# A two-layer graph kernel: 16-bit row pick, a reordered prologue, one-hots of two slots per compare in a ring of six, and PSUM banks by chunk size

## The reference

```
# layer 0
h = x @ W + b_W;  xi, xj = split(h)
m = xj[src] + (edge_attr @ W_e + b_We);  m = m / (in_degree[dst] + 1e-6)
x = layernorm(x + xi + segment_sum(m, dst))
# layer 1: graph convolution with self loops
h = x @ W1;  deg = in_degree + 1
out = segment_sum(h[src] * rsqrt(deg[src]) * rsqrt(deg[dst]), dst) + self loop + b
y = (out - mean(out)) * rsqrt(var(out) + eps) * gamma + beta   # over all nodes
x = layernorm(x + leaky(y, 0.01))
```

## Time and profile before

| | |
|---|---|
| timed runs, median of 3 | 941.71 us (941.57 to 946.58) |
| profiled execution, its own time | 944.12 us |
| its span | 942.3 us, TensorE clock granted 0.986 of full speed in the mean |
| TensorE busy | 892.4 us (95%), 12,235 matmul records |
| VectorE busy | 704.6 us (75%), 1,638 instructions |
| ScalarE busy | 458.9 us (49%) |
| GpSimd busy | 329.6 us (35%) |
| chain that ended last | TensorE 80%, VectorE 11%, issue 4%, ScalarE 3% |
| line 608, lo_oh | 391 instructions, 271.6 us, mean 695 ns |
| line 611, key_oh | 391 instructions, 235.8 us, mean 603 ns |

### The profile page before, as it was taken

The page is one execution under the profiler, slowest core; times in us unless marked ns, Lnnn a source line. Parts: engine busy times, 40 slices in busy tenths (PEclk is TensorE's granted clock), DMA queues, the critical chain, the costliest instruction groups (busy, mean ns, idle before and its releaser), DMA issues.

```text
span 942.3 us, 30938 instructions
## 1 busy us (share of the span) xinstructions
PE 892.4 (95%) x12235; PEld 796.3 (85%) x12235; DVE 704.6 (75%) x1638; ACT 458.9 (49%) x983; POOL 329.6 (35%) x401
## 2 busy tenths in 40 slices
PE   5768998999999999999999999999999999999995
PEld 4657887988988998989999999999988888888864
DVE  6999899999999998998888998888852111112255
ACT  4755665656665665565565565566542000000035
POOL 2224444555434453554343454344432010111100
PEclk9979999999999999999999999999999999999998
DMA  6428989897877887777687659687667897779645
GB/s 178 109 98 301 373 312 326 293 327 269 317 271 285 315 308 242 254 231 235 234 291 244 234 152 332 210 290 248 229 213 310 323 358 290 266 259 326 247 123 165
DMA packets 96765, 244.76 MB, mean 260 GB/s; under 512 B 42632, under 2 KB 64838, under 8 KB 90726
## 3 DMA queue, kind: packets, MB, share of 16 engines
q1 hardware_dynamic: 94150, 239.03, 72.2%
q0 software_dynamic: 1600, 3.28, 1.1%
q10 hardware_dynamic: 864, 0.39, 0.2%
HBM read 183.82 MB, written 58.85 MB: 258 GB/s over the span
## 4 chain that ended last, share of the span: by engine, by line
PE 80%; DVE 11%; issue 4%; ACT 3%; DMA 1%; SPq 1%; ACTq 0%; DVEq 0%
PE x_ps L868 23%; PE pair_ps L943 18%; PE pair_ps L850 12%; PE e_ps L887 9%; PE x_ps L876 9%; DVE key_oh L611 3%; DVE lo_oh L608 3%; PE j_ps L925 2%; PE pair_ps L952 1%; PE j_ps L926 1%; PE j_ps L973 1%; DMA counts_kept<-counts 1%; DVE streams L631 1%; PE u_vps L1401 1%; ACT counts L1053 1%
## 5 line engine op out<-in xcount | busy, mean ns | idle before, releaser
L1053 ACT CAST counts<-pair_ps 128x784 bf16<-128x784 f32 x391 | 314.6, 817 | 263.2 <-PE pair_ps L850 258.7
L868 PE MATMUL x_ps<-counts,xsplit 128*128 128x256 bf16 (+1 forms) x2450 | 307.8, 271 | 1.4 <-issue 1.4
L608 DVE TENSOR_TENSOR lo_oh<-counter,lo_t 128x1024 bf16<-128x1024 bf16 x391 | 271.6, 695 | 42.6 <-PE pair_ps L850 37.7
L868 PEld LDWEIGHTS x_ps<-counts,xsplit 128*128 128x128 f16 x2450 | 222.1, 98 | 31.4 <-issue 9.2
L611 DVE TENSOR_TENSOR key_oh<-counter,key_t 128x800 bf16<-128x800 bf16 x391 | 235.8, 603 | 0.0
L850 PE MATMUL pair_ps<-key_oh,lo_oh 128*128 128x100 bf16 x3128 | 207.3, 208 | 22.8 <-ACT counts L1053 13.5
L850 PEld LDWEIGHTS pair_ps<-key_oh,lo_oh 128*128 128x128 bf16 x3128 | 181.0, 98 | 39.3 <-DVE key_oh L611 17.2
L887 PE MATMUL e_ps<-streams 128*32 128x128 f32 x3528 | 108.8, 277 | 0.0
L876 PE MATMUL x_ps<-counts,zown 128*128 128x256 bf16 (+1 forms) x840 | 105.8, 269 | 0.0
L887 PEld LDWEIGHTS e_ps<-streams 128*32 128x32 f32 x3528 | 94.9, 111 | 4.9 <-issue 0.7
L943 PE MATMUL pair_ps<-streams,zown 128*128 128x256 bf16 x878 | 99.0, 273 | 0.0
(11 more groups left out here) (179 smaller groups left out, 866.0 us busy)
## 6 DMA issues: line engine op xcount, KB each, us to landing
streams<-in_edge_attr SPq DMA_DIRECT2D x196, 576.0 KB, 10.4
counts_kept<-counts SPq DMA_DIRECT2D x10, 1600.0 KB, 8.4
streams<-counts_kept SPq DMA_DIRECT2D x6, 1600.0 KB, 6.4
counts<-counts_kept SPq DMA_DIRECT2D x4, 1600.0 KB, 6.4
counts_kept<-counts SPq DMA_DIRECT2D x2, 3136.0 KB, 12.5
streams<-counts_kept SPq DMA_DIRECT2D x2, 3136.0 KB, 14.5
edst<-in_dst SPq DMA_DIRECT2D x196, 4.5 KB
streams<-in_x SPq DMA_DIRECT2D x3, 1024.0 KB, 5.4
```

What stands on the lines that cost most here:

```text
L608: dv.tensor_tensor(lo_oh[:, at % RING, :, :, :], counter[:, :, :].unsqueeze(1).to_broadcast([P, SW // 2, P, 2]), pairs(lo_t[b % 2][:, w]). ...
L868: last = nc.tensor.matmul(x_ps[:, 0, 0:n], xsplit[:, q // 2, q % 2, :], by_hi[:, q // 2, :], start=(q == 0), stop=(q == 2 * HS - 1))
L1053: a.copy(out.rearrange("p h (g n) -> p h g n", g=2), pair_ps[at % 2][:, :, 0:4 * KW].rearrange("p g (n h) -> p h g n", h=HI)[:, 0:HS]).the ...
```

## The change

- **Compares.** one_hots is called for every second s and writes both slots of the pair in one instruction per table: lo_oh 128x2048 and key_oh 128x1600. The semaphore "hot" counts pairs. The ring has 6 slots. TensorE's count, of one slot, waits for the pair that holds it.
- **Row pick.** Rows have 128 edges (HR = 128) and start at any edge. float_rows writes two tensors: the first and last element of each row in fp32 (heads, 128x2), and the row's 128 elements in bf16. The pick matrix is bf16, and find_rows is one bf16 product of 128x129.
- **Prologue.** Only the rows of blocks 0 and 1 are picked before the own products. Rows 2 and 3 are picked later: on ScalarE after own_out(2), on VectorE after make_keys(0), on TensorE after turn_keys(0). The weights are loaded by SP: wi ahead of the first piece of x, the others behind rows 2 and 3. count(0, 0) waits for two starts, count(0, 1) for four.
- **Memory.** early_in and dinv_row lie in the memory of key_oh. So the first two loads of dinv_row are issued after SP's loop and behind a wait for the last count.
- **The end.** Nine chunks have fixed places in PSUM and in the x1 buffers by their size. Five add_x1 stand ahead of add_leaky(0); add_x1(5) comes behind add_leaky(3), 6 behind 4, 7 and 8 behind 5. x1 loads are all issued before the first store.

```diff
-RING = 4
+RING = 6
-HR = 125
-R = E // HR
-ROW_MARGIN = 31
+HR = 128
+ROW_SPAN, ROW_MARGIN = P * HR, 4096
+def hot_pairs(at):
+    return -(-at // 2)
-        rows = [sb(f"rows{i}", [P, HR + 2], F32) for i in range(2)]
+        rows = [sb(f"rows{i}", [P, HR + 1], BF16) for i in range(2)]
+        heads = [sb(f"heads{i}", [P, 2], F32) for i in range(2)]
-        pick = [sb(f"pick{i}", [P, P], F32) for i in range(2)]
+        pick = [sb(f"pick{i}", [P, P], BF16) for i in range(2)]
+        spare = key_oh[:, :, :, :, :].rearrange("p r w k t -> p (r w k t)").bitcast(F32)
+        early_in, dinv_row = ([spare[:, BN * i:BN * (i + 1)] for i in k] for k in ((2, 3), (4, 5)))
...
             for b in range(2):
                 load_rows(sp, b)
+            sp.dma_start(wi, W0[:, 0:F]).then_inc(S["wi_in"], 16)
             load_inputs(sp, {"x": xf}, x, S, range(1))
             for b in range(2, ROW_RING):
                 load_rows(sp, b)
+            load_weights(sp, {"wj": wj, "we": we, "bi": bi, "bj": bje, "be": be_t[:, :]}, W0, b0, We, be, S)
             sp.wait_ge(win_in[0], 32)
...
                     sp.wait_ge(S["dinv_kept"], 16 * NB)
-                    for i in range(2):
-                        load_inverse(i)
...
+            sp.wait_ge(S["built"], first_slot(NB - 1) + slots(NB - 1))
+            for i in range(2):
+                load_inverse(i)
             load_early(1)
...
-                at = first_slot(b) + s
-                reach(dve, S["built"], at + 1 - RING)
-                w = slice(SW * s, SW * (s + 1))
+                at, n = first_slot(b) + s, min(2, slots(b) - s)
+                reach(dve, S["built"], at + n - RING)
+                w, g = slice(SW * s, SW * (s + n)), SW // 2 * n
+                ring = slice(at % RING, at % RING + n)
-                dv.tensor_tensor(lo_oh[:, at % RING, :, :, :],
-                                 counter[:, :, :].unsqueeze(1).to_broadcast([P, SW // 2, P, 2]),
-                                 pairs(lo_t[b % 2][:, w]).to_broadcast([P, SW // 2, P, 2]), ALU.is_equal)
+                dv.tensor_tensor(lo_oh[:, ring, :, :, :].rearrange("p r w k t -> p (r w) k t"),
+                                 counter[:, :, :].unsqueeze(1).to_broadcast([P, g, P, 2]),
+                                 pairs(lo_t[b % 2][:, w]).to_broadcast([P, g, P, 2]), ALU.is_equal)
...
             for b in range(2):
                 count_row(b)
                 start_of(b)
-                find_below(b + 2)
-                pick_rows(b + 2)
             ready_own_weights()
-            dve.wait_ge(S["consts"], CONSTS)
             dv.memset(total[:, :], 0.0)
             step(dv.tensor_copy(ebase[:, :], ebase_i[:, :]))
+            largest(0)
+            make_keys(0)
+            for b in range(2, 4):
+                find_below(b)
+                pick_rows(b)
             for b in range(2, 4):
                 count_row(b)
                 start_of(b)
-            largest(0)
-            make_keys(0)
...
-                    if b < NB and s < slots(b):
+                    if b < NB and s < slots(b) and s % 2 == 0:
                         one_hots(b, s)
...
-                pe.wait_ge(S["hot"], at + 1)
+                pe.wait_ge(S["hot"], hot_pairs(at + 1))
...
-            for b in range(4):
+            for b in range(2):
                 find_rows(b)
...
             turn_keys(0)
+            for b in range(2, 4):
+                find_rows(b)
             own_product(OWN_FIRST - 1)
-            pe.wait_ge(S["starts_known"], 4)
+            pe.wait_ge(S["starts_known"], 2)
...
-                a.activation(rows[b % 2][:, 0:HR + 1], (rows_i[b % ROW_RING] if b < LATE else late_rows_i)[:, :],
-                             ACT.Identity, bias=shift[:, b:b + 1]).then_inc(S["rows_float"], 1)
+                given = (rows_i[b % ROW_RING] if b < LATE else late_rows_i)
+                a.activation(heads[b % 2][:, :], given[:, 0:HR + 1:HR], ACT.Identity, bias=shift[:, b:b + 1])
+                a.activation(rows[b % 2][:, 0:HR], given[:, 0:HR], ACT.Identity, bias=shift[:, b:b + 1])\
+                 .then_inc(S["rows_float"], 1)
...
             for b in range(2):
                 float_rows(b)
-            load_weights(act, {"wi": wi, "wj": wj, "we": we, "bi": bi, "bj": bje, "be": be_t[:, :]}, W0, b0, We, be, S)
-            for b in range(2, 4):
-                float_rows(b)
             for m in range(OWN_FIRST):
                 x_turned(m)
                 if m >= 1:
                     own_out(m - 1)
+            for b in range(2, 4):
+                float_rows(b)
             tables(0)
...
+    AHEAD = 5
+    X1_HOME = ((0, 0), (0, 2), (1, 0), (2, 0), (3, 0), (0, 0), (1, 0), (2, 0))
+    V_HOME = ((0, 0), (0, 4), (1, 0), (2, 0), (3, 0), (0, 0), (1, 0), (2, 0), (2, 4))
+    HOME_LEFT = {5: 2, 6: 3, 7: 4, 8: 4}
+    ADD_AFTER = {3: (5,), 4: (6,), 5: (7, 8)}
...
-                for c in range(VB):
+                for c in range(AHEAD):
                     add_x1(c)
                 pe.wait_ge(U["center_ready"], 2 * turn + 2)
                 for c in range(LC + 1):
                     add_leaky(c)
-                    if VB <= c + 2 <= LC:
-                        add_x1(c + 2)
+                    for n in ADD_AFTER.get(c, ()):
+                        add_x1(n)
```

More of the change, by code:

```diff
@@ L114, in first_row @@
 def first_row(b):
-    return max(0, min(b * BN * E // (N * HR) - ROW_MARGIN, R - P))
-LATE = min(b for b in range(NB) if first_row(b) == R - P)
-assert all(first_row(b) + P < R for b in range(LATE))
+    return max(0, min(b * BN * E // N - ROW_MARGIN, E - ROW_SPAN))
+LATE = min(b for b in range(NB) if first_row(b) == E - ROW_SPAN)
 def early(k):
@@ L253, in layers @@
         s1 = [s1_mem[:, 2 * i:2 * i + 2, :].rearrange("f a n -> f (a n)") for i in range(2)]
-        dinv_row, early_in = ([sb(f"{n}{i}", [P, BN], F32) for i in range(2)] for n in ("dinv_row", "early_in"))
         early_sum = s1
@@ L549, in find_below @@
                 reach(dve, S["picked"], b)
-                dv.tensor_scalar(below[:, :], even[:, :], rows[b % 2][:, 0:1], None, ALU.is_gt).then_inc(S["below"], 1)
+                dv.tensor_scalar(below[:, :], even[:, :], heads[b % 2][:, 0:1], None, ALU.is_gt).then_inc(S["below"], 1)
             def pick_rows(b):
@@ L554, in pick_rows @@
                 reach(dve, S["found"], b - 1)
-                dv.scalar_tensor_tensor(out=pick[b % 2][:, :], in0=even[:, :], scalar=rows[b % 2][:, HR:HR + 1],
+                dv.scalar_tensor_tensor(out=pick[b % 2][:, :], in0=even[:, :], scalar=heads[b % 2][:, 1:2],
                                         in1=below[:, :], op0=ALU.is_le, op1=ALU.mult).then_inc(S["picked"], 1)
@@ L988, in _ @@
                 for s in range(SL):
+                    if b == 0 and s == 1:
+                        pe.wait_ge(S["starts_known"], 4)
                     if b < NB and s < slots(b):
@@ L1239, in finish_rows @@
         r = [sb(f"r{i}", [P, C * F], F32) for i in range(RB)]
-        v_ps = [ctx.enter_context(nc.psum_tensor(f"u_vps{i}", [P, C, F], F32)) for i in range(VB)]
+        v_ps = [ctx.enter_context(nc.psum_tensor(f"u_vps{i}", [P, C, F], F32)) for i in range(4)]
         def form(turn, passed):
```

72 lines of the change are left out of this document (35 added, 37 removed).

## The result

The changed kernel took 937.18 us in the median (935.51 to 938.37; one execution of 2256 us, far from all others, is left out), the kernel before beside it 941.76. The ratio is 0.9943 (0.9928 to 0.9959): 5.4 us faster by the ratio, 4.6 by the medians, against 13.2 us forecast. A second session gave 0.9936 (0.9916 to 0.9956). The sign was right and the size too large by a factor of more than two. The time (937.2) lies inside the range by 0.3 us, since the range had been drawn to hold the first rival too.

What follows compares the result with a forecast made beforehand. TensorE was taken to bind blocks 12 and later, VectorE blocks 1 to about 8. +0.3 - 3.8 - 6.2 - 3.1 - 0.6 = -13.4 us gave 930.7 us profiled, 928.5 timed; range 920.5 to 937.5.

Steps and rivals of the forecast that it cites:

- the first rival: Whole kernel: TensorE alone binds, compares and ring give nothing, only row picks and the end gain: -5.7 us, 936; chance 0.15.
- the pair's and the ring's term: Blocks 1 to 10: paired compares and a ring of six return time lost to VectorE's pace, -3.8 and -6.2 us.
- Row pick: Each block's find_rows in 16 bits saves 0.23 us of TensorE; -3.1 us where TensorE binds, blocks 10 to 21.
- Blocks 1 and 2: 48 to 119.86 us, into block 3: VectorE's 2.2 us saved plus 1.6 us of its idle, -3.8 us (0 to -6).
- Blocks 3 to 10: Block 3 to block 10, s = 4: 181.9 us falls toward 173.6; three quarters taken, -6.2 us (-1.6 to -8.3).
- the 8.0 down to about 2: Sign to look for: TensorE's idle time in 100 to 300 us falls from 8.0 us to about 2.
- The ring: Six slots instead of four cover bursts of TensorE and VectorE; four ready slots last 7 us; gain summed with the pairs.
- Prologue: Up to 48 us: one-hots start at 20.2, first count loses 1.5 us, not lasting; +0.3 us (-1 to +1.5).
- Blocks 11 on: Late blocks, where TensorE binds: 12 row picks give 2.7 us, half the idle in 300 to 400 us 0.4; -3.1 us.
- End: End stage: add_x1(4) ahead of leaky(0), so leaky(3) starts 1.2 us sooner; -0.6 us (+0.8 to -1.5).
- GpSimd: All blocks: longer waits behind paired compares, zscale's mean up to 2.5 to 3 us, covered by 13.6 us slack a block.

Runs made afterwards that it cites:

- b_keep: Kernel before with the store of block 0's counts issued ahead of block 1's edge loads: 939.01 us, ratio 0.9973 to the kernel before.
- a_keep: Changed kernel with the store of block 0's counts issued ahead of block 1's edge loads: 931.14 us, ratio 0.9890 to the kernel before.
- the repeat: Second profile of the kernel before, nothing altered: own time 942.62 us, span 940.7 us.
- a_half: Changed kernel without the lo_oh compare of every second slot (probe, counts not the reference's): 935.34 us, ratio 0.9930 to the kernel before.
- a_single6: Changed kernel with compares made for one slot at a time, ring of six kept: 938.50 us, ratio 0.9958 to the kernel before.
- a_single4: Changed kernel with compares for one slot at a time and a ring of four: 938.54 us, ratio 0.9955 to the kernel before.
- a_warm2: Changed kernel with idle matmuls filling TensorE's waits in the prologue: 937.84 us, ratio 0.9962 to the kernel before.

## Why the prediction was right in sign and wrong in size

The step that failed is the pair's and the ring's term, -3.8 and -6.2 us: it took TensorE's and VectorE's idle time in blocks 1 to 10 for time that VectorE's pace costs, and most of it was not. The rest of the sum was off by some 2.5 us, most of it in the prologue.

1. **Row pick** (-3.1, and 1.6 within the -6.2): right. 0.23 us a block by forecast, 28.18 to 27.99 or less by tables; undoing it costs 3.9 to 4.7 us.
2. **Blocks 1 and 2** (-3.8, measured -1.0 and -2.2): failed. The sum took VectorE's 2.2 us and 1.6 us of its idle time as if block 2 could begin when VectorE let it. Block 2 begins when a 3.1 MB store has landed, and the store's issue hangs on SP's chain, which the change doesn't touch. VectorE's idle time of that stretch was the gate's: in b_keep it is gone with nothing but the store moved. The row was in the trace of before, 2.79 us ahead of 87.82, named "issue"; I passed over it. With the gate open the change is worth 7.9 us instead of 6.1, and tables(4) comes 1.8 us earlier in a_keep than in b_keep: some 2 of the missing 8 us are the gate's, not all.
3. **Blocks 3 to 10** (-6.2, measured -3.4 and -5.0, of it 1.6 the row pick's): mis-sized. I compared 181.9 us with 173.6 and saw it confirmed by 8.0 us of TensorE's idle. Of the repeat's 8.2, only 2.3 wait for key_oh; 3.3 are pair_out's at the blocks' heads and 2.3 one "issue" whose cause stays open. The earlier trace rows holds a total over 48 to 300 us, and most of its 12.9 us lay before 100. The forecast wanted the 8.0 down to about 2; the changed kernel has 6.2, and a_half, with 104 us of VectorE's work gone and no key_oh wait left in 100 to 300 us, still 5.6. Its tables(4) to tables(11), 178.3 us, lies between the two profiles of the changed kernel (179.0 and 177.4): VectorE has nothing more to give there that could be told from scatter.
4. **The ring** was costed as a gain (it carries one engine past the other's bursts). With single compares its worth can't be told from nothing (-0.3 us by the ratios with the gate shut, 1.1 with it open), with pairs it is 51 us: a condition of the pairs, which my working named (slot five back) but did not turn round.
5. **Prologue** (+0.3, measured +1.0 to +2.0 at tables(2)): mis-sized. The one-hots started at 19.44, not 20.2, and the first count at 21.71, not 22.3. What I had not counted is the microsecond lost behind it, between the copies of slots 0 and 2, where the granted clock is 0.64 and with the old prologue 1.00. It isn't made up later, since with either prologue slots 2, 3 and 4 follow at 2.34 us each: the engines' own pace begins at slot 2, not at slot 5.
6. **Blocks 11 on** (-3.1, measured -2.2): 0.17 us a block instead of 0.23, and the half of the idle in 300 to 400 us did not come back; it is 1.3 us (100 less 98.67 in the stretches), where it had been 0.9. **End** (-0.6): right, 0.5 to 0.8.
7. **GpSimd**: the price fell where I had not looked. Two rows that answer to the earlier trace rows, changed kernel:

```profile
L484 POOL TENSOR_SCALAR zscale<-quot 128x2 f32<-128x2 f32 x25 | 7.6, 303 | 1.7
...
L485 POOL TENSOR_SCALAR dinv<-quot 128x2 f32<-128x2 f32 x25 | 27.2, 1087 | 1.6
```

zscale's mean is 303 ns, not 2.5 to 3 us, and dinv pays instead. GpSimd is 20.5 us busier in all. Over the 25 blocks it still waits 232.0 + 81.0 us for VectorE, where the earlier trace rows had 220.6 + 119.9: its slack is 12.5 us a block, and nothing shows that it decided anything, as forecast.

Two slips of arithmetic change nothing: 941.71 less 13.4 is 928.3, not 928.5, and TensorE's need in block 6 comes to 24.4 us, not 24.5.

The rival "TensorE alone binds, compares and ring give nothing" said 936 with a chance of 0.15. It has the better number, and for blocks 3 to 10 nearly the mechanism: row pick and end are worth 4.6 to 5.4 us. Its number is in part luck, since the compares do give something, 1.4 to 1.7 us with the gate shut and 3.5 to 4.2 with it open, and the prologue takes about 1 back. What it misses is that VectorE's saving exists and is held up at one store.

## What to carry to other kernels

Before a faster engine's time is credited, list who else TensorE waits for in that very stretch, by total, and follow the first instruction of the next block on every engine: a buffer guarded by a store's landing swallows a gain made before it, and a wait named "issue" is one to explain, not to pass over. A ring has to hold the unit being written plus what the reader needs meanwhile, so doubling the unit needs the larger ring first. And one profiled execution of a kernel may hold 2 us of its own: a second one is worth having when the forecast is of 1%.

## What the runs showed of the chip

- A 3.1 MB store took 11.5 us from issue to landing beside the edge loads (10.9 to 12.7 in twelve profiles) and 9.5 us with the DMA engines idle before it (a_keep, issue at 52.72 us, and b_keep).
- Two GpSimd instructions of the same shape (128x2), which run while VectorE compares, change their length with the compares: zscale takes 2087 to 2539 ns in the mean and dinv 246 to 280 with single compares (the kernel before twice, a_single6, a_single4), zscale 303 and dinv 1087 with pairs, and dinv 601 where the lo_oh compare is half as long (a_half).
- In a_warm2, with TensorE's granted clock at 1.00 over 20 to 28 us where the changed kernel had 0.64, ScalarE's copies behind it came 0.9 us earlier. That the clock alone did it is not shown.
